# A time-warping front stage on Trainium2: where its norms are made, and in how many pieces its distances come

## The chip, the cores and the metric

The kernel runs on one core of a Trainium2 chip. The metric is device time in microseconds (us) from the first to the last instruction of one launch; the reported time is a median of several runs, beside one profiled execution from which all rows are taken. The engines are TensorE (PE, with its weight loads as PEld), VectorE (DVE), ScalarE (ACT), GpSimd (POOL) and SyncE (SP, which here only issues DMAs).

## The reference

The layer has four residual steps. Only the first is touched here: it aligns the context (4 batches of 1024 rows, 256 wide) with the layer-normed x (4 batches of 512 rows, 256 wide) by dynamic time warping.

```python
x = x + tanh(g_xattn[0]) * align(ctx_1024, layernorm(x))        # per batch:
    D = sqrt(max(aa + bb - 2 * small @ large.T, 0))               # small = ctx, large = normed x
    R[i, j] = D[i, j] + min(R[i-1, j], R[i, j-1], R[i-1, j-1])    # (1024, 512), in order
    path = backtrack(R)                                           # diagonal, up, left
    out[j] = sum of ctx rows on the path in column j
x = x + tanh(g_ffn[0]) * (attention, then mixture of experts)(layernorm(x))
x = x + tanh(g_xattn[1]) * cross_attention(layernorm(x), ctx_1024, mask)
x = x + tanh(g_ffn[1]) * fp4_ffn(layernorm(x))
```

Here `aa` and `bb` are the squared norms of the context rows and of the normed x rows.

## The kernel before

`load_all` brings in x and the context and turns the context so that its 256 features lie along partitions (`ctxT`). `dtw_block` (L159) then runs five blocks, and each ends with all engines waiting for each other:

1. `layer_norm` "ln0" (L51): DVE computes mean and variance of 16 groups of 128 rows, ACT takes the root, DVE writes the normed x.
2. `transpose_tokens` "xT" (L86): PE turns it, and it is kept times -2 as `xnT`.
3. `dtw_norms` (L181): twelve jobs of 512 columns. DVE squares (L234), PE sums the squares over partitions with a two-column weight (L248), DVE copies the sums out (L206). Eight jobs give the context norms, which go through DRAM (`ctx_norms`, L215 and L217) to be laid out as `norms`, one value per partition and row; four jobs give the norms of x, `rows_j`.
4. `dtw_costs` (L253): the distances and the recurrence.
5. `backtrack`.

In `dtw_costs` each partition holds a block of 33 context rows of one batch (32 blocks by 4 batches). The distances are made in pieces of up to 112 columns of x (`cuts`, L294). A piece has 33 tiles, one for each row of a block. For a tile PE does eight products (two halves of the features by four batches, each batch in its own 32 columns of the array, L333) and four more with two-row weights that add the norm of x (L336). A product of float32 is two instructions. Four PSUM banks take tiles in turn. Of the first piece DVE adds the context norm and clips at zero (L357) and ACT takes the root (L460). For all later pieces ACT does both: `rectify` (L449) for each tile, then four `root` (L456) over the piece, then `store` (L439) to `dist` in DRAM. Two SBUF buffers take the pieces in turn.

The recurrence walks 576 skewed columns in 36 chunks of 16 (`CH`). SP loads a chunk (L316) when the piece that holds it is stored (L313) and the chunk's buffer is free (L315), that is, just after the first column of the chunk before it. For each column DVE does a minimum (L378), a shuffle (L383) and a scan (L389), with pieces of `rule` (L348 to L351) between them that say which way the path came. After each chunk ACT copies these results out in `keep` (L430, L432). DVE may start the rules of chunk n only when ACT's `keep` of chunk n-2 is done (L403).

ACT's order of work is fixed in L463 to L473: in the chunks n = 0, 1, 2 of every four, eleven `rectify` ahead of the `keep` of that chunk; in the fourth, four `root` and the `store`.

```python
q, turn = 1 + n // 4, n % 4
if q < len(cuts) and turn < 3:
    for k in range(11):
        rectify(q * RB + 11 * turn + k)
elif q < len(cuts):
    for i in range(4):
        root(q, i)
    store(q)
act.wait_ge(coded, n + 1)
keep(1 - n % 2, n * CH)
```

Of the kernel before, what the change touches and what calls it, by code (L numbers as in the profile page):

```python
# [26 lines left out]
WIDE = 112  # L27
ITILE = SK // P
# [130 lines left out]
def dtw_block(nc, d, x_sb, ident, ctxT, ctxT_d):  # L159
# [3 lines left out]
    norms_d = nc.dram_tensor("ctx_norms", [1, B * PADI], F32).ap()  # L163
    with ExitStack() as es:
        near = es.enter_context(nc.sbuf_tensor("near", [P, RB, TROW], F16))
        above = es.enter_context(nc.sbuf_tensor("above", [P, RB, TROW], F16))
        with ExitStack() as es1:
            xnT = es1.enter_context(nc.sbuf_tensor("xnT", [P, DH, B * S], F32))
            with ExitStack() as es2:
# [4 lines left out]
            rows_j = es1.enter_context(nc.sbuf_tensor("rows_j", [2, B, S], F32))  # L174
            norms = es1.enter_context(nc.sbuf_tensor("norms", [P, RB], F32))
            dtw_norms(nc, d, xnT, ctxT, rows_j, norms, norms_d)
            dtw_costs(nc, d, dist, near, above, xnT, ctxT, ctxT_d, rows_j, norms, x_sb)
# [3 lines left out]
def dtw_norms(nc, d, xnT, ctxT, rows_j, norms, norms_d):  # L181

    with ExitStack() as es:
        sq = es.enter_context(nc.sbuf_tensor("sq", [P, 2, 2, 512], F32))
        ones2 = es.enter_context(nc.sbuf_tensor("ones2", [P, 2, 2], F32))
        add2 = es.enter_context(nc.sbuf_tensor("add2", [2, 2], F32))
        rows_i = es.enter_context(nc.sbuf_tensor("rows_i", [2, B, PADI], F32))
        ps_n = [es.enter_context(nc.psum_tensor(f"ps_n{i}", [P, 512], F32)) for i in range(2)]
        consts = es.enter_context(nc.semaphore("d_consts"))
        squared = es.enter_context(nc.semaphore("squared"))  # L190
        normed = es.enter_context(nc.semaphore("normed"))
        norm_kept = es.enter_context(nc.semaphore("norm_kept"))
        filled = es.enter_context(nc.semaphore("d_filled"))
        stored = es.enter_context(nc.semaphore("d_norms_stored"))
        spread = es.enter_context(nc.semaphore("d_norms_spread"))

        jobs = [(0, b, c, 1.0) for b in range(B) for c in range(0, SK, 512)] + [(1, b, 0, 0.25) for b in range(B)]
        with nc.Block() as block:
            def keep_norm(dve, n):
                w, b, c, f = jobs[n]  # L200
                if n == 0:
                    dve.wait_ge(consts, 32)
                    dve.wait_ge(filled, 2)
                dve.wait_ge(normed, n + 1)
                dst = rows_j[:, b, :] if w else rows_i[:, b, LEAD + c:LEAD + c + 512]
                nc.vector.tensor_scalar(dst, ps_n[n % 2][0:2, :], add2[:, w:w + 1], None,  # L206
                                        ALU.add).then_inc(norm_kept, 1)

            @block.sync
            def _(sp):  # L210
                sp.dma_start(ones2[:], d["c_ones2"]).then_inc(consts, 16)
                sp.dma_start(add2[:], d["c_add2"]).then_inc(consts, 16)
                sp.wait_ge(norm_kept, 2 * B)
                sp.wait_ge(filled, 2)
                sp.dma_start(norms_d, rows_i[0:1, :, :].rearrange("o b i -> o (b i)")).then_inc(stored, 16)  # L215
                sp.wait_ge(stored, 16)
                sp.dma_start(norms[:, :], norms_d.rearrange("o (p r) -> (o p) r", r=RB)).then_inc(spread, 16)  # L217
                sp.wait_ge(spread, 16)

            @block.gpsimd  # L220
            def _(pool):

                nc.gpsimd.memset(rows_i[:, :, :], 1.0).then_inc(filled, 1)
                pool.wait_ge(filled, 1)
                nc.gpsimd.memset(rows_i[0:1, :, 0:LEAD], FAR2).then_inc(filled, 1)

            @block.vector
            def _(dve):
                for n, (w, b, c, f) in enumerate(jobs):
                    if n >= 2:  # L230
                        dve.wait_ge(normed, n - 1)
                    for h in range(DH):
                        src = xnT[:, h, b * S:(b + 1) * S] if w else ctxT[:, b, h, LEAD + c:LEAD + c + 512]
                        i = nc.vector.scalar_tensor_tensor(sq[:, n % 2, h, :], src, f, src, ALU.mult, ALU.mult)  # L234
                    i.then_inc(squared, 1)
                    if n >= 1:
                        keep_norm(dve, n - 1)
                keep_norm(dve, len(jobs) - 1)

            @block.tensor  # L240
            def _(pe):
                pe.wait_ge(consts, 32)
                for n, (w, b, c, f) in enumerate(jobs):
                    pe.wait_ge(squared, n + 1)
                    if n >= 2:
                        pe.wait_ge(norm_kept, n - 1)
# [6 lines left out]
def dtw_costs(nc, d, dist, near, above, xnT, ctxT, ctxT_d, rows_j, norms, x_sb):  # L253
# [8 lines left out]
    with ExitStack() as es:  # L262
# [32 lines left out]
        with nc.Block() as block:  # L295
# [129 lines left out]
            def _(act):  # L425
# [36 lines left out]
                for n in range(NCH):  # L462
# [4 lines left out]
                    elif q < len(cuts):  # L467
                        for i in range(4):
                            root(q, i)
# [1819 lines left out]
```

## Time and profile before

| | us |
|---|---|
| median of 3 runs (2691.69 to 2695.81) | 2692.8 |
| profiled execution, its own time | 2694.47 |
| its span from first to last instruction | 2692.7 |

Of the span PE is busy 66%, DVE 61%, ACT 36%, POOL 10%. These shares are means over stages with different limits. The part that is touched lies in the first 510 us; the chain of work that ended last, on the page, is far behind it in the feed-forward step, and so the rows below are taken by stage.

### The profile page before, as it was taken

To read this page: it belongs to the slowest core of one execution; us is meant where nothing else is said; L and a number is where in the kernel's file an instruction comes from. 1 tells how busy PE (TensorE), PEld (TensorE's weight loads), DVE (VectorE), ACT (ScalarE), POOL (GpSimd) and SP (SyncE) were. 2 spreads that over 40 slices of the span, in tenths; PEclk is the share of its full clock that TensorE was granted. 3 is DMA by queue.
4 is the path that set the end of the run, shared out by engine and by line. 5 is a ranking of instruction groups with operands and counts; after the bars stand their busy time and mean duration, and the time that the engine had idled before them with its cause. 6 is when DMAs were issued, how large, how long until landed. Compare 5 with 4: busy or idle time off the path is not lost. (4 is left out here: it accounts for less than half of the span.)

```text
span 2692.7 us, 39964 instructions
## 1 busy us (share of the span) xinstructions
PE 1789.7 (66%) x13193; PEld 1032.5 (38%) x13272; DVE 1647.0 (61%) x6787; ACT 982.2 (36%) x1794; POOL 260.3 (10%) x224
## 2 busy tenths in 40 slices
PE   5989500170837888832979507999999999604675
PEld 2445300010724555421656405444544543303453
DVE  5397899898658888440101146767667676286544
ACT  1244522220015666500212002666666666313322
POOL 0000000000000000013000220000000000064432
PEclk8555555555958999955989857999999999857888
DMA  3211100300010000025041122100100000100000
GB/s 96 110 61 51 70 28 28 109 0 1 16 45 9 9 9 2 1 81 192 24 146 49 49 78 86 55 2 1 56 1 25 1 1 1 33 0 0 0 0 31
DMA packets 60244, 104.90 MB, mean 39 GB/s; under 512 B 7449, under 2 KB 42703, under 8 KB 58407
## 3 DMA queue, kind: packets, MB, share of 16 engines
q1 hardware_dynamic: 42654, 72.91, 7.9%
q10 hardware_dynamic: 14352, 22.28, 2.3%
q0 software_dynamic: 3072, 7.53, 0.9%
q8 instruction: 100, 1.64, 0.3%
q14 instruction: 66, 0.54, 0.1%
HBM read 70.72 MB, written 32.85 MB: 38 GB/s over the span
## 5 line engine op out<-in xcount | busy, mean ns | idle before, releaser
L1026 DVE CUSTOM_DVE_ANT_0 xam_junk<-xam_s,xa_mask_q 128x512 bf16<-128x512 f32 x512 | 339.7, 687 | 170.2 <-PE xam_s L933 169.6
L1099 ACT ACTIVATE xam_exp<-xam_s 128x512 f32<-128x512 f32 x512 | 299.6, 598 | 204.1 <-PE xam_s L967 167.6
L933 PE MATMUL xam_s<-xa_kT,xa_qT 96*128 96x512 bf16 x512 | 198.4, 391 | 16.6 <-DVE xam_max L1026 11.1
L964 PE MATMUL xam_s<-xa_qT,xa_kT 99*128 99x512 bf16 x512 | 196.9, 385 | 14.2 <-ACT xam_exp L1099 13.3
L635 PE MATMUL ps_e<-near,start_terms 128*128 128x512 f16 x66 | 27.7, 420 | 211.8 <-DMA lag<-c_lag 204.5
L967 PE MATMUL xam_s<-xa_mask_k,identb 128*128 128x512 bf16 x433 | 165.2, 381 | 0.0
L389 DVE TENSOR_TENSOR_SCAN cost<-m,cost,dist_chunk 128x33 f32<-128x33 f32 x576 | 164.1, 285 | 0.0
L333 PE MATMUL ps_d<-xnT,ctxT 128*32 128x112 f32 (+1 forms) x2640 | 151.5, 379 | 18.0 <-ACT stage L449 7.9
L1026 DVE CUSTOM_DVE_ANT_0 l0m_junk<-l0m_s,l_tri_q 128x128 bf16<-128x128 f32 (+3 forms) x256 | 118.7, 488 | 42.8 <-PE l0m_s L933 40.1
L978 PE MATMUL xam_o<-xam_exp,xa_vt 128*32 128x512 f32 x1024 | 137.2, 605 | 0.0
L1548 PE MATMUL ex_up<-ex_xT,ex_w 128*128 128x512 f32 x256 | 117.0, 616 | 17.6 <-DVE ex_xT L1580 12.0
L1099 ACT ACTIVATE l0m_exp<-l0m_s 128x512 f32<-128x512 f32 (+3 forms) x256 | 104.1, 439 | 60.9 <-PE l0m_s L967 59.3
L378 DVE TENSOR_TENSOR m<-cost 128x33 f32<-128x33 f32 x576 | 109.4, 190 | 20.8 <-DMA dist_chunk<-dist 14.0
L850 POOL COPY l_stk<-l_stk 128x256 bf16<-128x256 bf16 x32 | 21.0, 657 | 1012.1 <-DVE l_stk L829 1012.1
L1580 DVE TENSOR_SCALAR ex_xT<-ex_t,moe_vecs 128x512 f32<-128x512 f32 x16 | 12.2, 805 | 171.7 <-PE ex_t L1535 96.6
L333 PEld LDWEIGHTS ps_d<-xnT,ctxT 128*32 128x32 f32 x2640 | 90.6, 161 | 68.2 <-issue 45.9
L1559 PE MATMUL ex_dn<-ex_w,ex_hm 128*128 128x256 f32 x512 | 111.5, 379 | 0.0
L964 PEld LDWEIGHTS xam_s<-xa_qT,xa_kT 99*128 99x128 bf16 x512 | 50.7, 99 | 140.4 <-ACT xam_exp L1099 99.5
L933 PE MATMUL l0m_s<-l_kT,l_qT 96*128 96x128 bf16 (+3 forms) x256 | 79.8, 317 | 36.0 <-DVE l0m_max L1026 25.9
L1559 PEld LDWEIGHTS ex_dn<-ex_w,ex_hm 128*128 128x128 f32 x512 | 97.2, 191 | 13.6 <-issue 1.0
L430 ACT COPY near<-chunk_near 128x528 f16<-128x528 f16 x37 | 39.9, 1078 | 158.9 <-DVE chunk_near L351 157.3
L635 PEld LDWEIGHTS ps_e<-near,start_terms 128*128 128x128 f16 x66 | 6.8, 102 | 228.5 <-DMA lag<-c_lag 204.7
(324 smaller groups left out, 3900.4 us busy)
## 6 DMA issues: line engine op xcount, KB each, us to landing
dist_chunk<-dist SPq DMA_DIRECT2D x36, 264.0 KB
ex_w<-L_ffn_W ACTq DMA_DIRECT2D x8, 1024.0 KB, 15.1
ex_w<-L_ffn_W SPq DMA_DIRECT2D x8, 1024.0 KB, 16.3
xa_mask<-mask_BxSxS_ik SPq DMA_DIRECT2D x4, 2048.0 KB, 11.1
ctx_nat<-ctx ACTq DMA_DIRECT2D x4, 1024.0 KB, 14.5
x_sb<-x SPq DMA_DIRECT2D x2, 2048.0 KB, 12.3
ctxT_d<-ctxT SPq DMA_DIRECT2D x4, 1024.0 KB, 9.5
ctx_rows<-ctx SPq DMA_DIRECT2D x1, 4096.0 KB, 15.5
```

Source lines behind the costliest of these rows:

```text
L333: nc.tensor.matmul(o[b], ctxT[:, b, h, k:PADI:RB], xnT[:, h, b * S + a:b * S + z], start=(h == 0), stop=False, tile_position=(0, 32 * b))
L378: nc.vector.tensor_tensor(m[:, u, :], w[:, src, 0:RB], w[:, src, 1:PITCH], ALU.min).then_inc(minned[h], 1)
L389: nc.vector.tensor_tensor_scan(w[:, dst, 1:PITCH], m[:, u, :], step[h][:, s, :], w[:, dst, 0:1], ALU.min, ALU.add).then_inc(scanned[h], 1)
L430: nc.scalar.copy(near[:, :, bass.ds(at, CH)], kept_n[buf][:, :, :].rearrange("p s r -> p r s"))
L933: nc.tensor.matmul(ps1[n % 2][:, 0:w], qT[0:STK, slot(g, h), qt * P:(qt + 1) * P], kT[0:STK, slot(g, h), f * 512:f * 512 + w], start=True, ...
L964: nc.tensor.matmul(o[:, q0:512], kT[:, slot(g, h), kt * P:(kt + 1) * P], qT[:, slot(g, h), q0:512], start=True, stop=False)
L967: nc.tensor.matmul(o[:, q0:q0 + w], identb[:, :], heads.bias_k(g, kt), start=False, stop=True).then_inc(scored2, 1)
L978: nc.tensor.matmul(pso[32 * h:32 * h + 32, q0:512], vt[:, kt, slot(g, h), :], ebuf[n % NE][:, q0:512], start=(kt == 0), stop=(kt == kt_n - 1),
L1026: nc.vector.tensor_tensor_reduce(junk[:, n % NJ, 0:w], ps1[n % 2][:, 0:w], heads.bias_q(g, qt, f), 1.0, NEG * 4, ALU.add, ALU.max, mx[:, g ...
L1099: nc.scalar.activation(ebuf[at % NE][:, q0:512], ps2[at % 2][:, q0:512], ACT.Exp).then_inc(exped, 1)
L1548: last = nc.tensor.matmul(pu[k % 4][:, :], w1[i][:, h, c * P:(c + 1) * P], xT[i % 2][:, h, :], start=(h == 0), stop=(h == DH - 1))
L1559: last = nc.tensor.matmul(pd[k % 2][:, 0:D], hm[i % 2][:, c, t * P:(t + 1) * P], w2[i][:, c, :], start=(c == 0), stop=(c == FC - 1))
```

## The change

- `layer_norm` and the context half of `dtw_norms` become one block, `norm_inputs`. POOL squares the context (eight instructions of 128x1024), PE sums them with a weight that puts each batch's sum on its own partition (`c_which`), ACT copies the sums out, SP stores them and reads them back as `norms`; DVE does the layer norm in the same block. SP does not wait there for the read-back; DVE does, in `dtw_costs`.
- The squares of xnT are made at the head of `dtw_costs`, by four DVE instructions of 128x1024, after PE has been given the feature products of the first four tiles. PE sums them by sixteen instructions, ACT copies the sums to `rows_j` (4x512).
- The norm of x is added to a tile by one product with a 4x128 weight (`c_share`) for all batches, in place of four with 2x32 weights.
- `m` and `cost` are preset by POOL in place of DVE.
- The pieces are 48, 64, 80, 96, 112 and 112 columns wide. The first is stored in two parts, 16 and 32 columns.
- ACT's work on a piece is spread evenly over the chunks of the piece before it.

```diff
+WIDTHS = (48, 64, 80, 96, 112, 112)
+STORES = (0, 16, 48, 112, 192, 288, 400)
...
-                layer_norm(nc, es2, x_sb, xn, "ln0")
+                with ExitStack() as es3:
+                    norm_inputs(nc, es3, d, x_sb, xn, ctxT, which, rows_i, norms, norms_d, spread)
...
-            dtw_norms(nc, d, xnT, ctxT, rows_j, norms, norms_d)
...
+def norm_inputs(nc, es, d, x_sb, xn, ctxT, which, rows_i, norms, norms_d, spread):
...
+            sp.dma_start(which[:, :, :], d["c_which"]).then_inc(known, 16)
+            sp.wait_ge(filled, 1)
+            sp.wait_ge(kept, 2)
+            sp.dma_start(norms_d, rows_i[:, :]).then_inc(stored, 16)
+            sp.wait_ge(stored, 16)
+            sp.dma_start(norms[:, :], norms_d.rearrange("b (p r) -> (b p) r", r=RB)).then_inc(spread, 16)
...
+            for n, (b, h) in enumerate(jobs):
+                if n >= 4:
+                    pool.wait_ge(weighed, n - 3)
+                src = ctxT[:, b, h, LEAD:PADI]
+                nc.gpsimd.tensor_tensor(sq[:, n % 4, :], src, src, ALU.mult).then_inc(squared, 1)
...
+                pe.wait_ge(squared, n + 1)
+                for c in range(2):
+                    last = nc.tensor.matmul(ps[c][0:B, :], which[:, b, :], sq[:, n % 4, c * 512:(c + 1) * 512],
+                                            start=(n == 0), stop=(n == len(jobs) - 1))
+                last.then_inc(weighed, 1)
...
+            act.wait_ge(weighed, len(jobs))
+            for c in range(2):
+                nc.scalar.copy(rows_i[:, LEAD + c * 512:LEAD + (c + 1) * 512], ps[c][0:B, :]).then_inc(kept, 1)
...
+        for q in range(1, len(cuts)):
+            first, turns = cuts[q - 1][0] // CH - 1, WIDTHS[q - 1] // CH
+            items = [("rectify", q * RB + k) for k in range(RB)] + [("root", (q, i)) for i in range(4)] + [("store", q)]
+            for i, item in enumerate(items):
+                work[first + i * turns // len(items)].append(item)
...
-                    for b in range(B):
-                        last = nc.tensor.matmul(o[b], one_j[:, :], rows_j[:, b, a:z], start=False, stop=True,
-                                                tile_position=(0, 32 * b))
-                    last.then_inc(prod, 1)
+                def close(n):
+                    a, z = cuts[n // RB]
+                    nc.tensor.matmul(ps[n % 4][:, 0:z - a], share[:, :], rows_j[:, a:z], start=False,
+                                     stop=True).then_inc(prod, 1)
+                for n in range(4):
+                    tiles(n)
+                for b in range(B):
+                    pe.wait_ge(squared, b + 1)
+                    for h in range(DH):
+                        last = nc.tensor.matmul(ps_j[0:B, :], which[:, b, :], squares[:, b, h * S:(h + 1) * S],
+                                                start=(b == 0 and h == 0), stop=(b == B - 1 and h == DH - 1))
+                last.then_inc(normed, 1)
+                pe.wait_ge(told, 16)
+                pe.wait_ge(jnormed, 1)
+                for n in range(4):
+                    close(n)
+                for n in range(4, len(cuts) * RB):
+                    tiles(n)
+                    close(n)
...
-                nc.vector.memset(w[:, :, :], FAR).then_inc(blank, 1)
-                nc.vector.memset(m[:, :, :], FAR).then_inc(blank, 1)
+                for b in range(B):
+                    src = xnT[:, :, b * S:(b + 1) * S]
+                    nc.vector.scalar_tensor_tensor(squares[:, b, :].rearrange("p (h s) -> p h s", h=DH), src, 0.25, src,
+                                                   ALU.mult, ALU.mult).then_inc(squared, 1)
+                dve.wait_ge(spread, 16)
...
+                act.wait_ge(normed, 1)
+                nc.scalar.copy(rows_j[:, :], ps_j[0:B, :]).then_inc(jnormed, 1)
...
                 store(0)
+                prepare(-1)
                 for n in range(NCH):
...
+                    prepare(n)
                     act.wait_ge(coded, n + 1)
                     keep(1 - n % 2, n * CH)
```

`prepare(n)` does the items of `work[n]` in order.

## Rows read from the trace of the kernel before

**Rows 1.** Busy time of each engine by stage: start:end length, engines, clock, DMA.
```profile
46.50:75.50 29.00, 24.01 (x48) 3.35 (x48) 23.81 (x37) 0.00 (x0) 3.80 (x2) 0.94 0.01 1
75.50:124.10 48.60, 48.52 (x812) 26.35 (x816) 15.13 (x35) 13.43 (x33) 0.00 (x0) 0.50 0.28 111
124.10:137.60 13.50, 13.50 (x228) 7.22 (x232) 0.00 (x0) 4.18 (x10) 0.00 (x0) 0.50 0.42 163
137.60:509.30 371.70, 160.05 (x2928) 89.63 (x2928) 340.68 (x2970) 133.54 (x209) 0.00 (x0) 0.50 0.13 45
509.30:2692.70 2183.40, 1527.31 (x9089) 890.06 (x9168) 1246.96 (x3685) 821.13 (x1528) 255.98 (x217) 0.84 0.10 34
```

**Rows 2.** What DVE waited for in the loop: us in total, times, longest.
```profile
DVE best L348 <- ACT above L432: 24.2, 5, 5.9
DVE m L378 <- DMA dist_chunk<-dist: 14.0, 1, 14.0
```

**Rows 3.** Timeline of ACT in the loop: start, duration, line, shapes, idle before.
```profile
209.03 0.47 ACT L449 ACTIVATE x_sb<-ps_d,norms 128x112 f32<-128x112 f32 x1 [0.98 <-PE ps_d L336]
210.72 1.07 ACT L430 COPY near<-chunk_near 128x528 f16<-128x528 f16 x1
...
403.52 1.07 ACT L430 COPY near<-chunk_near 128x528 f16<-128x528 f16 x1 [7.74 <-DVE chunk_near L351]
...
422.82 1.07 ACT L430 COPY near<-chunk_near 128x528 f16<-128x528 f16 x1 [7.75 <-DVE chunk_near L351]
```

**Rows 4.** Timeline of PE: tiles of 112 columns, then of 64.
```profile
75.58 0.98 PE L333 MATMUL ps_d<-xnT,ctxT 128*32 128x112 f32 x16 [2.27 <-DMA one_j<-c_one_j]
76.50 0.60 PE L336 MATMUL ps_d<-rows_j,one_j 2*32 2x112 f32 x8
77.02 0.98 PE L333 MATMUL ps_d<-xnT,ctxT 128*32 128x112 f32 x16
...
276.71 0.66 PE L333 MATMUL ps_d<-xnT,ctxT 128*32 128x64 f32 x16
277.30 0.44 PE L336 MATMUL ps_d<-rows_j,one_j 2*32 2x64 f32 x8
277.67 0.66 PE L333 MATMUL ps_d<-xnT,ctxT 128*32 128x64 f32 x16
```

**Rows 5.** Timeline of the blocks ahead of the distances.
```profile
26.55 5.32 DVE L66 BATCH_NORM_STATS2 ln_stats<-x_sb 128x6 f32<-128x256 f32 x16 [1.01 <-PEq L48]
...
39.28 6.40 PE L118 MATMUL xT_ps<-ident,dtw_xn 128*128 128x128 f32 x32 [14.03 <-PEq L61]
...
46.63 2.50 DVE L234 SCALAR_TENSOR_TENSOR sq<-ctxT 128x512 f32<-128x512 f32 x4 [0.66 <-PEq L96]
...
48.23 5.29 PE L248 MATMUL ps_n<-sq,ones 128*2 128x512 f32 x8 [2.54 <-DMA add<-c_add]
...
53.93 3.74 PE L248 MATMUL ps_n<-sq,ones 128*2 128x512 f32 x8 [0.41 <-DVE sq L234]
...
66.30 0.23 SPq L215 DMA_DIRECT2D ctx_norms<-rows_i  x1
...
67.99 0.35 SPq L217 DMA_DIRECT2D norms<-ctx_norms  x1
```

**Rows 6.** POOL's products of two tensors by shape: count, busy us, mean ns.
```profile
L1905 POOL TENSOR_TENSOR ffq_sgn<-ffq_sgn,ffq_amax 128x1024 f32<-128x1024 f32 x4 | 10.8, 2689 | 0.0
...
L1901 POOL TENSOR_TENSOR ffq_v<-ffw_xn,ffq_inv 128x1024 f32<-128x1024 f32 x4 | 8.7, 2176 | 8.6 <-DVE ffq_inv L1876 8.6
```

**Rows 7.** Timeline: first store, first load, first column of the recurrence.
```profile
124.13 0.35 ACTq L439 DMA_DIRECT2D dist<-x_sb  x1
...
132.08 0.62 SPq L316 DMA_DIRECT2D dist_chunk<-dist  x1
...
137.63 0.20 DVE L378 TENSOR_TENSOR m<-cost 128x33 f32<-128x33 f32 x1 [13.96 <-DMA dist_chunk<-dist]
```

**Rows 8.** ACT's roots over a piece of 64 columns, grouped by shape.
```profile
L456 ACT ACTIVATE x_sb<-x_sb 128x528 f32<-128x528 f32 x4 | 2.2, 625 | 0.0
```

More of the change, by code:

```diff
@@ L173, in dtw_block @@
                 transpose_tokens(nc, es2, xn, lambda g, h: xnT[:, h, g * 512:(g + 1) * 512], ident, "xT", mul=-2.0)
-            rows_j = es1.enter_context(nc.sbuf_tensor("rows_j", [2, B, S], F32))
-            norms = es1.enter_context(nc.sbuf_tensor("norms", [P, RB], F32))
-            dtw_norms(nc, d, xnT, ctxT, rows_j, norms, norms_d)
-            dtw_costs(nc, d, dist, near, above, xnT, ctxT, ctxT_d, rows_j, norms, x_sb)
+            dtw_costs(nc, d, dist, near, above, xnT, ctxT, ctxT_d, which, norms, spread, x_sb)
@@ L178, in dtw_block @@
         backtrack(nc, d, near, above, spans, x_sb, ident)
[L181 to L246, printed above, removed]
-                    for h in range(DH):
-                        last = nc.tensor.matmul(ps_n[n % 2][0:2, :], ones2[:, w, :], sq[:, n % 2, h, :],
-                                                start=(h == 0), stop=(h == DH - 1))
-                    last.then_inc(normed, 1)
@@ L262, in dtw_costs @@
+def dtw_costs(nc, d, dist, near, above, xnT, ctxT, ctxT_d, which, norms, spread, x_sb):
     with ExitStack() as es:
@@ L456, in root, with prepare @@
                     nc.scalar.activation(part, part, ACT.Sqrt).then_inc(rooted, 1)
+                def prepare(n):
+                    for kind, arg in work[n]:
+                        if kind == "rectify":
+                            rectify(arg)
+                        elif kind == "root":
+                            root(*arg)
+                        else:
+                            store(arg)
                 for k in range(RB):
                     act.wait_ge(clipped, k + 1)
-                    nc.scalar.activation(stage[0][:, :, k], stage[0][:, :, k], ACT.Sqrt).then_inc(rooted, 1)
+                    nc.scalar.activation(stage[0][:, 0:WIDTHS[0], k], stage[0][:, 0:WIDTHS[0], k],
+                                         ACT.Sqrt).then_inc(rooted, 1)
                 store(0)
+                prepare(-1)
                 for n in range(NCH):
-                    q, turn = 1 + n // 4, n % 4
-                    if q < len(cuts) and turn < 3:
-                        for k in range(11):
-                            rectify(q * RB + 11 * turn + k)
-                    elif q < len(cuts):
-                        for i in range(4):
-                            root(q, i)
-                        store(q)
+                    prepare(n)
                     act.wait_ge(coded, n + 1)
```

102 lines of the change are left out of this document (77 added, 25 removed).

## The prediction

> **What bounds the kernel now.** I read the busy time by stage first [rows 1]. The part that changes ends at 509.3; the 2183.4 us behind it share no instruction with the edit, so I carry them over unchanged. Ahead of that point there are two kinds of lost time. Up to 137.6 the recurrence has not begun: the norms take 29.0 us, the first piece of distances 48.6 with PE busy for 48.52, and 13.5 go to its store and first load, DVE at zero. From 137.6 to 509.3 DVE carries the recurrence, busy for 340.7 of 371.7.
>
> The waits of DVE say what is lost inside the loop [rows 2]: 24.2 us for ACT's `keep`, in five waits; the 14.0 for the first load are the stretch ahead of the loop. ACT's timeline says why [rows 3]: eleven `rectify` stand in front of a `keep`, and each waits 0.98 us for PE. The reader is to see that ACT works 0.47 us for each tile and the rest of its time is PE's. Where nothing waits, two chunks take 422.82 - 403.52 = 19.30, so 9.65 each; 36 of them make 347.4, and with 24.2 that is the loop's 371.6.
>
> PE's price for a tile [rows 4]: 1.44 us at 112 columns (0.92 for the eight feature products, 0.52 for the four norm products), 0.96 at 64 (0.59 and 0.37). Through both goes 0.32 + 0.010 per column: 0.80 at 48, 1.12 at 80, 1.28 at 96.
>
> **The change part by part.** All from the profiled execution, whose own time is 2694.47, 1.7 above the median shown.
>
> *Norms ahead of the distances.* The new block starts where the layer norm did, 26.55 [rows 5]. Its longest chain is POOL's: eight products of 128x1024. Two rows bound one, 2.18 and 2.69 [rows 6]; I take 2.3, near the first, since both operands are one tile: 18.4 us, to 45.2 with the preset (bounds 44.2 and 48.3). The layer norm's 12.7 us on DVE (26.55 to 39.28) lie beside it; were POOL and DVE to hold each other up for all of DVE's last pass, about 5 us would be added. Behind POOL come the last four sums on PE, 1.9 (half of 3.74 for eight), two ACT copies of 512 columns at 0.6 (a 528-element row is 0.625 [rows 8]), and SP's store with the issue of the read-back, 67.99 + 0.35 - 66.30 = 2.0 [rows 5]: 50.3, and with a block turn 50.6. This block is 11.3 us later at its end than the layer norm was. SP no longer waits for the read-back; DVE does, ahead of its 33 clips, but it lands some 15 us before the first tile, so nothing queues there. The transposes keep 46.63 - 39.28 = 7.35: `dtw_costs` starts at 57.9.
>
> Then PE does four feature halves (4 x 0.48 = 1.9) while DVE squares (8 x 0.625 = 5.0 in four steps of 1.25). PE's sixteen sums take 7.5 at the full clock, 2.4 GHz (twice 3.74), and 13.6 at the half, 1.2 GHz (0.85 each); a first group of eight in 5.29 shows both levels [rows 5]. I take 7.5, since dense transposes run directly before. ACT's copy, for which all closes wait, costs 0.8: 68.4. Four feature halves are then already done, so it is as if tile 0 had begun at 66.5, where it began at 75.58: 9.1 gained (bounds 10 and 0, with POOL's rows and the clock's two levels). Presets moved to POOL free 1.9 us of DVE that PE's sums cover anyway; SP's copies of `ctxT` and the presets' DMAs moved 0.28 x 48.6 = 13.6 us' worth in the first piece's stretch [rows 1]; they start with the block at 57.9 and are done long before the first store.
>
> *The one close for four.* No row shows a 4x128 product between column tiles. The old norm products cost 0.15 us beyond their columns; below, that goes to nothing with two instructions for eight (-0.15 a tile). Above, two loads of 128 columns lie open: a transpose instruction with such a load and 128 columns takes 0.20 [rows 5], half of it load, so +0.2. I take no change, the tile as before, as the streamed columns are the same number.
>
> *The pieces.* Tile 33 ends at 66.5 + 33 x 0.80 = 92.9; clip, root and issue bring the store to 93.9. A store of 112 columns took 7.95 [rows 7]; for 16 columns I take 2.6 (in proportion 1.1, but even a small store takes 1.7 [rows 5]; above 7.95). The load takes 137.63 - 132.08 = 5.55. The loop starts at 102.0, not 137.6. Of these 35.6, 9.1 are the norms, 21.1 the narrower piece, 5.3 the store.
>
> Piece 1 must be there for chunk 3, due at 102.0 + 28.9 = 130.9. PE ends it at 92.9 + 33 x 0.96 = 124.6; the last `rectify` 0.5, four roots 2.5 [rows 8], a store of 64 columns 4.5 (in proportion), the load 5.55: 137.6. Chunk 3 is late by 6.7. Piece 2, for chunk 7, due at 176.2: 124.6 + 37.0 + 1.0 of PE waiting on ACT + 0.5 + 3.0 + 5.7 + 5.55 = 177.3, late by 1.1. Piece 3 comes 4 us early for chunk 12, pieces 4 and 5 early or just in time, since PE needs at most 7.9 us of a chunk's 9.65 from there on. `keep` is late no more: in chunk 0, the tightest, 26 tiles of piece 1 stand before it, to 92.9 + 26 x 0.96 = 117.9, and with 2.2 it is done at 120.1, where chunk 2 begins at 121.3; from chunk 2 on ten items or fewer stand before one. So the 24.2 go and 7.8 come.
>
> *Sum.* 102.0 + 347.4 + 7.8 = 457.2 for 509.3: 52.1 gained, 2642.4, or 2640.7 on the median. Forecast 2641.
>
> **Rivals.**
>
> *The clock stays up.* PE was all but fully busy on tiles of 32 columns at half clock for 48.6 us [rows 1], so these tiles don't raise it. But they began there just after PE had stood idle for 2.27 us [rows 4]; now they would follow dense sums closely, 0.9 us apart. If the clock holds through two pieces, tiles cost 0.40 and 0.48: tile 33 ends at 78.7, the loop starts at 87.9, piece 1 is in time, and 87.9 + 347.4 = 435.3: 2620. Against it: narrow tiles with DVE and ACT in turn leave gaps. The Trainium skill, "TensorE: Matmul & The Clock Gate", section "What's actually happening", says that the throttled state is the default and activity releases it; by that rule alone 2620 would be likely, but the 48.6 us above disagree with it for this kind of tile.
>
> *The close drains the array.* Each tile now changes from four column tiles to the whole array and back, 396 times. Price: both loads open, +0.2 a tile. By chunk 7 that is 99 x 0.2 = 19.8 on 177.3, so 197.1; the 29 chunks left take 279.9: 477.0, and about 2 at chunk 12: 2664. With half of it, 2654. Against it: the old pair changed between 128-row and 2-row weights as often, at 1.44 in all. The Trainium skill, "TensorEngine Tiling (Array Packing)", section "Key Properties", says that a change of tiling mode drains the engine; no row here shows such a drain by itself.
>
> *Slower than before.* Place: PE between the last feature product and the close of each tile. If a tile costs 0.45 more, pieces 0 to 4 end 165 x 0.45 = 74 us later on PE. Piece 4 without that: 66.5 + 33 x (0.80 + 0.96 + 1.12 + 1.28 + 1.44) + 5 + 0.5 + 3.9 + 7.95 + 5.55 = 274.2, and 18 chunks behind it, 173.7: 447.9. With 74 it is 522: 2707. It decides from (509.3 - 447.9) / 165 = 0.37 a tile, nearly twice what two open loads cost.
>
> *It doesn't do what it says.* The loop keeps waiting for `keep` as before, 24.2 for the 7.8: 2659. Against it: of 112 columns at most seven stand before a `keep`, not eleven, and PE runs four tiles ahead; but chunk 0 has 1.2 us to spare only.
>
> **How the numbers follow.** Forecast 54% (2632 to 2652, from the front's bounds and -0.15 to +0.05 a tile), clock up 21% (2614 to 2632), drain or late `keep` 20% (2652 to 2672), slower 4%, no change 1%. The range 2616 to 2663 holds the first, most of the second and over half of the third. What a measurement can tell from no change is 0.2%, 5.4 us; all but the last two cases are faster by more: faster 0.95, same 0.01, slower 0.04.
>
> **What would show it.** POOL's eight products near 2.3 us and ending near 45; transposes from near 50.6; the first close near 68.5; tiles 0.80 us apart in the first piece and 1.44 at 112 columns, clock 0.50; the first column at 102; DVE waiting for a load, not for ACT, about 7 us near chunk 3 and hardly at all later; loop end near 457. Tiles 0.40 apart show the clock's rival, 1.0 or more in the first piece the drain. I am wrong if tiles at 112 columns exceed 1.8 us, if DVE still waits over 15 us in the loop, or if the stretch behind the loop is not 2183 within 5.

## The result, and the profile after

The changed kernel takes 2671.66 us (median of 4 runs, 2668.73 to 2674.33) where the kernel before, run beside it, takes 2693.6: a ratio of 0.9918, 95% interval 0.9901 to 0.9935. That is 22 us faster; 52 were forecast, and 2671.7 lies above the range. The profiled execution is 2674.33 long. Its stages, to be read beside [rows 1] (start:end length, busy time of PE, PEld, DVE, ACT, POOL, clock, DMA share, GB/s):

```profile
53.70:62.81 9.11, 8.26 (x80) 2.47 (x81) 4.63 (x4) 0.57 (x1) 1.96 (x2) 1.00 0.67 266
62.81:95.00 32.19, 32.19 (x547) 26.09 (x547) 9.71 (x33) 9.24 (x33) 0.00 (x0) 0.54 0.23 92
95.00:102.50 7.50, 7.50 (x110) 5.77 (x110) 0.00 (x0) 2.27 (x6) 0.00 (x0) 0.50 0.40 146
102.50:472.80 370.30, 230.94 (x2846) 160.97 (x2845) 340.44 (x2970) 145.86 (x249) 0.00 (x0) 0.50 0.13 48
472.80:2672.20 2199.40, 1544.65 (x9168) 895.32 (x9168) 1247.38 (x3686) 822.31 (x1528) 255.69 (x217) 0.83 0.10 34
```

The loop starts at 102.5 (102.0 forecast) but takes 370.3 instead of 355.2, so it ends at 472.8 (457.2 forecast, 509.3 before), and the stretch behind it is 2199.4 instead of 2183.4, in code that the change doesn't touch. DVE still has 340.4 us of work in the loop; what it waits for is this, to be read beside [rows 2]:

```profile
DVE m L419 <- DMA dist_chunk<-dist: 26.1, 4, 9.6
DVE best L386 <- ACT above L475: 4.9, 1, 4.9
```

The 26.1 are 7.8 ahead of the loop, then 9.6, 6.9 and 1.8 for chunks 3, 7 and 12. The blocks ahead of the loop, beside [rows 5]:

```profile
26.47 14.99 POOL L222 TENSOR_TENSOR ctx_sq<-ctxT 128x1024 f32<-128x1024 f32 x8
34.51 10.97 DVE L249 TENSOR_SCALAR dtw_xn<-x_sb,ln_mv,ln_rstd 128x256 f32<-128x256 f32 x16
47.45 5.35 PE L120 MATMUL xT_ps<-ident,dtw_xn 128*128 128x128 f32 x32 [3.73 <-PEq L205]
55.03 7.03 PE L367 MATMUL ps_j<-x_sb,which_batch 128*4 128x512 f32 x16
62.81 0.39 PE L359 MATMUL ps_d<-rows_j,share 4*128 4x48 f32 x2 [0.76 <-ACT rows_j L469]
```

And a tile of 112 columns, beside [rows 4]:

```profile
301.98 0.98 PE L353 MATMUL ps_d<-xnT,ctxT 128*32 128x112 f32 x16
302.89 0.50 PEld L359 LDWEIGHTS ps_d<-rows_j,share 4*128 4x128 f32 x2 [0.33 <-issue]
302.89 0.76 PE L359 MATMUL ps_d<-rows_j,share 4*128 4x112 f32 x2
303.58 0.58 PEld L353 LDWEIGHTS ps_d<-xnT,ctxT 128*32 128x32 f32 x16 [0.20 <-issue]
303.58 0.98 PE L353 MATMUL ps_d<-xnT,ctxT 128*32 128x112 f32 x16
```

The close is what finishes a tile, the product of `share` that adds the norm of x. From the start of the features' products to the close it is 0.91 us, as before; the close takes 0.69 where the four took 0.52, so 1.61 a tile for 1.44. At 48, 64, 80 and 96 columns the tiles come 1.07, 1.21, 1.34 and 1.47 us apart: 0.27, 0.25, 0.22 and 0.19 more than forecast. Only the first six ran at the full clock, the fifth and sixth 0.74 apart; at 65.3 the granted clock fell to 0.50, and it stayed there for the rest of the loop.

### The profile page after: what moved, and what is told of

The parts are those of the page before. It is cut to its first block and busy times, and to the rows that moved or that the text cites. A ratio compares the mean times of both kernels' runs of the same rounds, so it can differ in the third digit from the quotient of the medians.

```text
span 2672.2 us, 39247 instructions
## 1 busy us (share of the span) xinstructions
PE 1854.2 (69%) x12876; PEld 1108.5 (41%) x12876; DVE 1629.2 (61%) x6753; ACT 991.3 (37%) x1834; POOL 273.3 (10%) x233
## 5 line engine op out<-in xcount | busy, mean ns | idle before, releaser
L1016 PE MATMUL xam_s<-xa_qT,xa_kT 99*128 99x512 bf16 x512 | 196.7, 384 | 13.7 <-ACT xam_exp L1151 12.9
L1019 PE MATMUL xam_s<-xa_mask_k,identb 128*128 128x512 bf16 x512 | 195.3, 381 | 0.0
L353 PE MATMUL ps_d<-xnT,ctxT 128*32 128x112 f32 (+4 forms) x3168 | 158.1, 348 | 9.8 <-ACT stage L497 8.4
L359 PE MATMUL ps_d<-rows_j,share 4*128 4x112 f32 (+4 forms) x396 | 140.5, 456 | 0.8 <-ACT rows_j L469 0.8
L1600 PE MATMUL ex_up<-ex_xT,ex_w 128*128 128x512 f32 x256 | 122.9, 641 | 21.9 <-DVE ex_xT L1632 12.6
L419 DVE TENSOR_TENSOR m<-cost 128x33 f32<-128x33 f32 x576 | 109.6, 190 | 32.6 <-DMA dist_chunk<-dist 26.1
L359 PEld LDWEIGHTS ps_d<-rows_j,share 4*128 4x128 f32 x396 | 96.9, 303 | 49.0 <-issue 45.7
L353 PEld LDWEIGHTS ps_d<-xnT,ctxT 128*32 128x32 f32 x3168 | 97.1, 160 | 40.1 <-issue 17.4
```

Source lines behind the costliest of these rows:

```text
L353: nc.tensor.matmul(ps[n % 4][32 * b:32 * b + 32, 0:z - a], ctxT[:, b, h, k:PADI:RB], xnT[:, h, b * S + a:b * S + z], start=(h == 0), stop= ...
L359: nc.tensor.matmul(ps[n % 4][:, 0:z - a], share[:, :], rows_j[:, a:z], start=False, stop=True).then_inc(prod, 1)
L419: nc.vector.tensor_tensor(m[:, u, :], w[:, src, 0:RB], w[:, src, 1:PITCH], ALU.min).then_inc(minned[h], 1)
L1016: nc.tensor.matmul(o[:, q0:512], kT[:, slot(g, h), kt * P:(kt + 1) * P], qT[:, slot(g, h), q0:512], start=True, stop=False)
L1019: nc.tensor.matmul(o[:, q0:q0 + w], identb[:, :], heads.bias_k(g, kt), start=False, stop=True).then_inc(scored2, 1)
L1600: last = nc.tensor.matmul(pu[k % 4][:, :], w1[i][:, h, c * P:(c + 1) * P], xT[i % 2][:, h, :], start=(h == 0), stop=(h == DH - 1))
```

## The experiments

Two questions: what makes the close dear, and where the 16 us behind the loop come from. "Stretch" is the time from the loop's last column to the end of the span.

**e1, four closes again.**

```
-                    nc.tensor.matmul(ps[n % 4][:, 0:z - a], share[:, :], rows_j[:, a:z], start=False,
-                                     stop=True).then_inc(prod, 1)
+                    for b in range(B):
+                        last = nc.tensor.matmul(ps[n % 4][32 * b:32 * b + 32, 0:z - a], share[:, 32 * b:32 * b + 32],
+                                                rows_j[:, a:z], start=False, stop=True, tile_position=(0, 32 * b))
+                    last.then_inc(prod, 1)
```

> The changed kernel with one edit: each tile of distances is closed by four products, one a batch, each of 32 columns of share (its four rows long) into its own 32 partitions, in place of one product of all 128 columns; everything else is as in the changed kernel. Theory (the whole-array product is what costs: its tile pitch was 1.07, 1.21, 1.34, 1.47 and 1.61 us at 48, 64, 80, 96 and 112 columns against 0.96 at 64 and 1.44 at 112 before): the pitch comes back to about 0.80, 0.96, 1.12, 1.28 and 1.44 us, the loop still starts near 102, its wait for chunk 3 falls from 9.6 to about 7 us and that for chunk 7 from 6.9 to about 1, and it ends near 450 instead of 472.8; the total is 2650, give or take 8 for the stretch behind the loop (2183 to 2199). Rival (the dearer tile comes from something else that changed in these pieces, for instance the sums of x in four rows instead of two, or the order of work on ScalarE): the pitch stays and the total is 2671.

Measured: 2650.1, tiles 0.80, 0.96, 1.12, 1.28 and 1.44 apart, loop 100.6 to 453.0, stretch 2195.7. At 112 columns:

```profile
291.83 0.98 PE L353 MATMUL ps_d<-xnT,ctxT 128*32 128x112 f32 x16 [2.53 <-ACT stage L499]
292.74 0.60 PE L360 MATMUL ps_d<-rows_j,share 4*32 4x112 f32 x8
293.27 0.98 PE L353 MATMUL ps_d<-xnT,ctxT 128*32 128x112 f32 x16
```

The whole-array close alone costs 19.8 us of loop end and 21.5 of the total. The stretch stays long, so the close is not its cause.

**e4, paired closes, and e6, closes of 64 columns.** In e4 `tiles(n); tiles(n + 1); close(n); close(n + 1)` replaces `tiles(n); close(n)`; in e6 the loop of e1 runs over two halves of 64 columns.

> The changed kernel with the products of each two tiles put together: eight products of features for tile n, eight for n+1, then the two closes, from the fifth tile on. The number and shape of the products stay. T1 (going over between products of 32 columns of the array and one of all its columns costs a fixed time, once each way): a pair pays it once instead of twice, and two tiles take 0.15 to 0.3 us less together than twice the pitch of now (2.95 at 48: about 1.95 to 2.0 instead of 2.15; at 112 about 3.0 instead of 3.21); the loop ends near 461. T2 (each close pays for loading its own 128 columns of weights before it, which nothing hides): the pair takes what two single tiles took, 2.15 at 48 and 3.21 at 112 within 0.05, and the loop ends within 2 of 472.8.

Measured: 2655.9, loop end 459.7. A pair takes 1.82 us at 48 columns and 2.78 at 112, which is 0.33 and 0.43 less than two tiles of the changed kernel: more than T1's 0.15 to 0.3, where T2 gave nothing. So a change of shape does cost something. But the second close of a pair adds 0.43 at every width, which T1 doesn't explain. Two closes at 112 columns, up to the next features:

```profile
303.02 0.93 PEld L359 LDWEIGHTS ps_d<-rows_j,share 4*128 4x128 f32 x4 [0.33 <-issue]
303.02 1.19 PE L359 MATMUL ps_d<-rows_j,share 4*128 4x112 f32 x4
304.14 1.33 PEld L353 LDWEIGHTS ps_d<-xnT,ctxT 128*32 128x32 f32 x32 [0.20 <-issue]
```

Each f32 product is two passes (two records a close), and from the second on they follow each other by 0.213 at 48 as at 112 columns: the columns streamed don't set this pace. The 128 columns of weights that each pass loads are the same at both widths; e6 tries whether it is they that do.

> The changed kernel with each tile closed by two products of 64 columns of share, one for each half of the partitions. The paired closes gave 0.213 us from pass to pass of a 128-column close whatever its width. T2' (what is paid is the loading of the close's columns: the first load lies open behind the features' products, the second sets the pitch of the second pass; 0.213 us for 128 columns at the low clock, so 0.107 for 64 and 0.053 for 32): a tile costs 0.05 more than with four closes, and at 48 columns 0.03 more, so 0.88, 1.01, 1.17, 1.33 and 1.49 us at 48, 64, 80, 96 and 112 columns; the loop ends near 457. T1 (what is paid is a fixed price of going from 32 columns to more and back): the tile stays near 1.07, 1.21, 1.34, 1.47 and 1.61 and the loop ends near 473.

Measured: 2653.2, loop end 454.6 (457 expected), tiles 0.87, 1.00, 1.16, 1.32 and 1.48 apart, where T2' gave 0.88 to 1.49 and T1 1.07 to 1.61.

```profile
293.54 0.98 PE L353 MATMUL ps_d<-xnT,ctxT 128*32 128x112 f32 x16 [2.33 <-ACT stage L499]
294.45 0.64 PE L360 MATMUL ps_d<-rows_j,share 4*64 4x112 f32 x4
295.02 0.98 PE L353 MATMUL ps_d<-xnT,ctxT 128*32 128x112 f32 x16
```

So what a close costs beyond its columns goes by the columns of weights loaded, as T2' has it: the first load lies open, the second holds the second pass back. The Trainium skill, "TensorE: Matmul & The Clock Gate", section "LDWEIGHTS (loading the stationary operand)", says that the load's time goes by the columns and not by the contracted rows; e1, e6 and the changed kernel, with 32, 64 and 128 columns, agree as to the columns; the rows were 4 in all three.

**e3, equal pieces** (WIDTHS 112, 112, 112, 112, 64, one store each, one close a tile) **and e8, the same with four closes.**

> The changed kernel with the pieces of before: 112, 112, 112, 112 and 64 columns, each stored by one transfer; norms and closes as in the changed kernel. Theory (the dear close takes back what the graded pieces bring): the first store leaves some 22 us later, the loop starts near 124.6 instead of 102.5, has no wait for a chunk any more, and ends near 471.6, within 3 of the changed kernel's 472.8; tile pitch 1.607 us at 112. Total 2655 to 2672 by the stretch behind the loop (2183 to 2199). Rival (the graded pieces still bring what they were forecast to, about 30 us): the loop ends near 500.

Measured: 2662.0, loop 125.0 to 472.0 without a wait. The changed kernel's loop ends at 472.8: under the dear close the graded pieces bring nothing. Yet this kernel is 9.6 us faster, nearly all of it behind the loop (2189.8).

> The changed kernel with the pieces of before (112, 112, 112, 112 and 64 columns, one store each) and four closes a tile: of the change only the norms and their place are left. Expected from the two single edits: tile pitch 1.44 at 112 columns, loop start 119.5 (125.0 with equal pieces and one close, less 33 tiles by 0.167), no wait for a chunk, loop end 466.5. The graded pieces are then worth 13.5 us with four closes (466.5 to 453.0) and nothing with one (472.0 and 472.8). Rival (the start of the loop is not set by the tiles but by ScalarE's and VectorE's own work on the first piece): loop start 124 or later. Total 2650 to 2665 by the stretch behind the loop; if equal pieces are what keeps that stretch short (2188 with them, 2194 to 2197 with graded pieces), 2656.

Measured: 2653.4, loop 123.2 to 469.9 (119.5 and 466.5 expected), stretch 2184.7. So the norms' new place and ScalarE's new work list, which this kernel keeps too, bring 39 us of loop end: 14 by the earlier start, and 25 in the loop, where no `keep` is waited for any more, although the pieces and the tile's 1.44 us are as before. The likely reason is the work list, which here puts five or six items ahead of each `keep`, where eleven tiles stood ahead of three in four; no run has the one without the other. The graded pieces add 17 with four closes.

**e2 and e5, a pause behind the loop.** A block in which VectorE fills 2048 columns of a scratch tensor, in the changed kernel and in the kernel before.

> The changed kernel with an idle block between the loop and the walk back: VectorE fills 2048 columns of a scratch tensor (about 1.8 us at the rate of the 1920-column fill, 1658 ns, plus the ends of a block), and all the other engines wait. No work is changed in what follows. Theory P (the 16 us that the code behind the loop took longer, 2199.4 against 2183.4 us, come from when its matmul bursts fall against the changes of TensorE's granted clock, so that they move with any delay): the stretch behind the loop, less the pause, comes out several us away from 2199.4, in either direction, and the total with it. Rival (the change costs the code behind it a fixed amount, by something it leaves behind): the stretch less the pause is 2199.4 within 2 and the total is the changed kernel's plus the pause, 2674 to 2676.

> The kernel before with the same idle block between the loop and the walk back as in the paused changed kernel (VectorE fills 2048 columns of a scratch tensor). In the runs so far the stretch behind the loop, the median time less what lies ahead of it, is 2182.6 us before, 2196.7 in the changed kernel, 2195.0 with four closes a tile, 2194.1 with paired closes, 2188.2 with equal pieces. Theory P (the stretch depends on when its matmul bursts fall against the changes of the granted clock): a shift alone makes it longer here too, by 3 us or more beyond the pause, median 2699 or more. Rival (something in the changed kernel makes it longer, whatever the shift): the kernel before keeps its 2183 and becomes 2696 (2693.84 and the pause of 2.3) within 2.

Measured: 2674.2 (2670.8 to 2683.6) and 2696.9 (2695.0 to 2700.7). By the medians a shift costs little more than it lasts, 2.6 and 3.5 us; the long stretch doesn't go away in the one or come in the other. So theory P doesn't explain why the stretch is long. The four runs of e2 lie 13 us apart, though, so some scatter of this kind is there.

**e9, seven stores, and e11, five on ScalarE's queue.** In the traces so far the stretch was long in the kernels with graded pieces and seven stores, and most of the time was lost in the experts' stage, where ScalarE issues sixteen transfers of weights ahead of its gelu, in two groups of eight ("issues" below is the time that each group takes to issue). e9 is e8 with STORES = (0, 16, 112, 224, 336, 400, 448).

> The kernel of e8 (equal pieces, four closes a tile) with seven stores of distances in place of five: cut also at columns 16 and 400, as many transfers as the changed kernel sends by ScalarE's queue. The traces of all five kernels with seven stores show the eight pairs of weight transfers of the experts' stage (2.3 MB, issued on ScalarE's queue 800 us later) issued in 24.8 to 26.2 us, and those of the four kernels with five stores in 21.4 to 23.6 us; gelu waits for the last issue, TensorE for gelu. Theory Q (the number of stores on ScalarE's queue decides how its later issues are held up): the issues take 25 us, the stretch behind the loop goes from 2184.7 to 2194, the loop ends near 469 and the total is 2664. Rival R (it is the number of tiles or the length of the program, 198 tiles against 161 or 165): the issues stay at 22 us, the stretch at 2185, the total at 2654. Rival P (only the time at which the bursts fall against the changes of the clock): either, but without the change in the issues.

Measured: 2662.6, loop end 466.0, issues 24.6 and 25.7 us, stretch 2194.9: theory Q. e11 is the changed kernel with two stores moved from ScalarE to SyncE (shortened):

```
+   sp.wait_ge(rooted, RB)          # SyncE, ahead of the first load
+   sp.dma_start(dist[:, ...], stage[0][...]).then_inc(stored[j], 16)    # j = 0 and 1
```

> The changed kernel with the two stores of the first piece (columns 0 to 16 and 16 to 48) issued by SyncE in place of ScalarE: seven stores as before, five of them on ScalarE's queue. Loop start 102.5 and loop end 472.8 within 1.5. Theory Q1 (the number on ScalarE's own queue decides): the experts' weights on ScalarE's queue are issued in about 22 us in the pattern of five stores (5, 10 and 4 us at the fourth, sixth and eighth), the stretch behind the loop is about 2186, and the total 2660. Theory Q2 (the number of store transfers in all decides, on whichever queue): the issues take 25 us, the stretch stays at 2195 to 2199 and the total at 2671.

Measured: 2658.7, loop 101.8 to 472.2, issues 23.3 and 21.3, stretch 2184.5: theory Q1 (2186 and 2660 expected). The second group of weights on ScalarE's queue in the changed kernel (start, time of the issue), then in e11:

```profile
1361.62 4.48 ACTq L1567 DMA_DIRECT2D ex_b<-L_ffn_b  x1
1366.26 0.66 ACTq L1564 DMA_DIRECT2D ex_w<-L_ffn_W  x1
1367.08 4.69 ACTq L1567 DMA_DIRECT2D ex_b<-L_ffn_b  x1
1371.94 6.59 ACTq L1564 DMA_DIRECT2D ex_w<-L_ffn_W  x1
1378.68 6.40 ACTq L1567 DMA_DIRECT2D ex_b<-L_ffn_b  x1
1385.18 1.28 ACT L1576 ACT_TABLE_LOAD   x1 [57.78 <-issue]
```

```profile
1353.09 4.61 ACTq L1576 DMA_DIRECT2D ex_b<-L_ffn_b  x1
1357.86 0.39 ACTq L1573 DMA_DIRECT2D ex_w<-L_ffn_W  x1
1358.41 8.08 ACTq L1576 DMA_DIRECT2D ex_b<-L_ffn_b  x1
1366.66 1.46 ACTq L1573 DMA_DIRECT2D ex_w<-L_ffn_W  x1
1368.28 4.38 ACTq L1576 DMA_DIRECT2D ex_b<-L_ffn_b  x1
1372.75 1.28 ACT L1585 ACT_TABLE_LOAD   x1 [53.89 <-issue]
```

ScalarE is held in its own eight issues for 25.2 us (from 1359.87) instead of 21.3 (from 1351.34), so its gelu starts late, and TensorE, whose four banks of products are full, waits (changed kernel, then e11; idle before in brackets; the last row of each is the stretch behind the wait, with PE, PEld, DVE, ACT, POOL, granted clock and DMA):

```profile
1373.31 10.18 PE L1600 MATMUL ex_up<-ex_xT,ex_w 128*128 128x512 f32 x16 [4.54 <-DVE ex_xT L1632]
1387.21 6.19 PE L1600 MATMUL ex_up<-ex_xT,ex_w 128*128 128x512 f32 x7 [3.72 <-ACT ex_hm L1576]
1387.20:1393.40 6.20, 6.19 (x8) 2.69 (x9) 0.00 (x0) 2.38 (x4) 0.00 (x0) 0.52 0.63 201
```

```profile
1364.25 8.65 PE L1609 MATMUL ex_up<-ex_xT,ex_w 128*128 128x512 f32 x16 [4.26 <-DVE ex_xT L1641]
1374.79 5.42 PE L1609 MATMUL ex_up<-ex_xT,ex_w 128*128 128x512 f32 x12 [1.89 <-ACT ex_hm L1585]
1374.80:1380.20 5.40, 5.40 (x13) 2.53 (x14) 0.00 (x0) 3.04 (x5) 0.00 (x0) 1.00 1.09 351
```

It waits 3.7 instead of 1.9, and behind the longer wait its products run at a granted clock of 0.52 and 0.88 us apart (7 in 6.19), behind the shorter at 1.00 and 0.45 apart (12 in 5.42). From the first issue of this group to the end of the span the changed kernel takes 1312.3 us and e11 1305.4. The first group loses in the same way: from its first issue to that of the second it is 143.5 and 140.4.

**e10 and e12, six and four stores on ScalarE's queue.** e10 is the changed kernel without the cut at 16, e12 is e8 with its first store issued by SyncE.

> The changed kernel with its first piece stored by one transfer of 48 columns instead of two of 16 and 32: six stores. The loop starts some 1 us later (the store of 48 columns lands 3.4 us after its issue, that of 16 after 2.1) and ends at 472 to 474. Theory Q: the stretch behind the loop changes by some microseconds from 2196.7, in a direction that five and seven stores don't tell; the issues of the experts' weights show another pattern than 4.9, 6.7 and 5.8 us. Rival R: the same pattern, 2196.7 and a total of 2671 to 2673.

> The kernel of e8 (equal pieces, four closes a tile, five stores) with the first store issued by SyncE: four stores on ScalarE's queue. Loop end 470. Theory Q1: the issues of the experts' weights show a third pattern; their sum may be 22 or 25 us (five gave 22, six, seven and eight gave 25), and if the rule is 'few are good' it stays at 22 with a total of 2653. Theory Q2 (five in all): 22 us, the pattern of five stores, 2653.

Measured: e10 2671.4, loop end 471.7, issues 25.5 and 25.5 in another pattern (the longest single issue 10.3 us, 6.7 in the changed kernel), stretch 2198.1; e12 2658.5, loop end 465.5, issues 24.7 and 24.5, stretch 2190.8. Few is not good: with four, six and seven the issues take 25 us, with five 22. Two further versions, both with four closes, give eight and five:

> Seven pieces of 48, 48, 64, 64, 80, 96 and 112 columns, eight stores, four closes a tile of 32 columns, the products of two tiles put together: an attempt at a faster version. The loop starts at 100.6 as with paired tiled closes (there ScalarE's and VectorE's own work on the first piece takes over from TensorE), has no wait and ends near 447.5. By theory Q the stretch behind it is not known for eight stores: 2184 to 2196, total 2634 to 2646.

> Five pieces of 80, 96, 112, 112 and 112 columns, five stores, four closes a tile: the graded start with as few stores as before. The loop starts near 111, has no wait for a chunk and ends near 458. Theory Q: with five stores the experts' weights are issued in 22 us and the stretch is 2184.7, total 2645. Rival R (198 tiles or the graded pieces decide; here there are 165 tiles): also 2645; rival P: 2645 to 2655.

Measured: best2 2640.7, loop 97.2 to 444.4, issues 25.7 and 24.8, stretch 2199.3; best4 2645.6, loop 114.0 to 461.1 (111 to 458 expected), issues 22.8 and 21.7, stretch 2186.9. The kernel before happened to stand at five. Why five, no run shows.

The stretch is read best in two parts, up to the first of these issues (at 1247.40 in the kernel before, 1216.33 in the changed one, 1210.98 in e11) and from it to the end of the span:

| | stores on ScalarE's queue | loop end to first issue | first issue to end |
|---|---|---|---|
| before | 5 | 738.1 | 1445.3 |
| e8 | 5 | 739.1 | 1445.6 |
| e11 | 5 | 738.8 | 1445.7 |
| best4 | 5 | 741.3 | 1445.7 |
| e3 | 5 | 741.4 | 1448.4 |
| e12 | 4 | 738.2 | 1452.6 |
| e9 | 7 | 739.2 | 1455.7 |
| changed kernel | 7 | 743.5 | 1455.9 |
| e10 | 6 | 742.1 | 1456.0 |
| best2 | 8 | 743.3 | 1456.0 |

The second part goes by the stores, about 10 us between five and six or more. The first does not: with seven stores it is as short as 739.2 (e9), with five as long as 741.4 (e3). Of the 16.0 us by which the changed kernel's profile is longer behind the loop, 10.6 belong to the queue; the other 5.4 lie ahead of these issues, where the traces scatter, and what makes them scatter is open.

**e7 and the versions built on it.** e7 is e1 with the tiles in pairs.

> The changed kernel with four closes a tile (32 columns each) and the products of each two tiles put together: features of n and n+1, closes of n and n+1, from the fifth tile on. In the trace with four closes a tile takes six passes of w/600 us and 0.32 us besides, of which the trace shows 0.15 to 0.16 at each of two places, into the close and out of it. Theory (the 0.16 is paid where products of one shape follow products of another, so that it is there in the kernel before too): a pair takes 12 passes and 0.32 once: 1.28, 1.60, 1.92, 2.24 and 2.56 us at 48, 64, 80, 96 and 112 columns, the loop starts near 95 and ends near 440, and the total is 2638 give or take 6. Rival (the 0.16 belongs to each accumulation group, that is to each tile): a pair takes 1.60 to 2.88 and the loop ends near 453 as with four closes.

Measured: 2645.2, loop 100.6 to 447.5. Pairs come 1.28 to 2.56 apart, as in the theory, so 0.16 is paid at each change from products of one shape to another, and most likely in the kernel before too, whose tile of 1.44 is that of e1. But the loop starts 5 late: the first close comes at 65.5 (62.8 in the changed kernel), and TensorE stops for 3.95 in the first piece. It also stops in the same kernel with two stores by SyncE:

> The changed kernel's pieces and seven stores with four closes a tile and paired tiles (2645.2 with loop end 447.5), its first two stores issued by SyncE, five on ScalarE's queue. Loop end 447 to 448. Theory Q1: weights issued in 22 us, stretch 2186, total 2635. Theory Q2: 25 us, total 2645.

Measured: 2632.1, loop 97.2 to 444.0, issues 22.9 and 21.3, stretch 2185.5. Its TensorE in the first piece:

```profile
64.60 0.34 PE L362 MATMUL ps_d<-xnT,ctxT 128*32 128x48 f32 x6
68.90 0.80 PE L362 MATMUL ps_d<-xnT,ctxT 128*32 128x48 f32 x26 [3.97 <-issue]
70.10 0.88 PE L362 MATMUL ps_d<-xnT,ctxT 128*32 128x48 f32 x32
```

It stops amid the features of a pair, with nothing to wait for that the profile shows, while the copy of the transposed context (4 MB) fills the DMA engines. From 65 to 69 they are 96% busy with it (packets, MB, share of the 16 engines):

```profile
q1 hardware_dynamic: 409, 1.55, 96.1%
q8 instruction: 1, 0.02, 1.5%
```

The second row is a queue that brings instructions. A third version of this kind missed its loop end:

> The version with seven graded pieces, eight stores, four closes a tile and paired tiles (2640.7 with loop end 444.4 and 2199 behind it), with its first three stores issued by SyncE, so that five stay on ScalarE's queue. Loop end 444 to 446. Theory Q1: weights issued in 22 us, stretch 2186, total 2631. Theory Q2: 25 us, 2195 to 2199, total 2641.

Measured: 2636.2, stretch 2184.2 as expected, but loop end 448.5: SyncE, waiting to send the third store, is late with chunk 2's load, and VectorE waits 5.3 us.

The last version is the one of 2632.1 with that copy moved behind the loads of chunks 26, 28, 30 and 32.

> The version with paired tiles and five stores on ScalarE's queue (2632.1; loop 97.2 to 444.0), with the four transfers that copy the transposed context to memory (1 MB each) moved from ahead of the loop to behind the loads of chunks 26, 28, 30 and 32. In six traces with closes in tiles TensorE stood still for 2.3 to 4.0 us in the first piece, waiting for nothing but instructions, until about when these transfers ended. Theory: its instructions come by transfers that queue behind them; without them the stop of 3.97 us goes, the loop starts near 93.2, has no wait and ends near 440, total 2628. Rival (the stop is of the program itself): it stays, the loop ends near 444, total 2632; a chunk load held up by the moved copies would show as a wait of VectorE behind chunk 26.

Measured: 2627.1, ratio 0.9753 (0.9737 to 0.9769), loop 92.9 to 440.0 with no wait in it, and no stop (here the window of the view ends at 66.5, within the last row):

```profile
64.77 1.26 PE L363 MATMUL ps_d<-xnT,ctxT 128*32 128x48 f32 x32
66.44 0.32 PE L363 MATMUL ps_d<-xnT,ctxT 128*32 128x48 f32 x4
```

So the copy causes the stop. That TensorE waits for its instructions is the likely way, as the instructions' queue brings nothing from 60 to 65 with the copy there and one packet of 16 KB without it; no run tests it by itself.

**e13, the changed kernel with both cures.**

> The changed kernel with both single cures: four closes of 32 columns a tile, and the two stores of the first piece issued by SyncE (five on ScalarE's queue). If the two causes add up and there is no third: loop end 453.0, stretch behind it 2184.5, total 2639.6 give or take 3, against the forecast of 2641 made without either. If they overlap or a third cause is there, the total is 2645 or more.

Measured: 2641.0 (2638.1 to 2644.2), loop 97.8 to 452.0, stretch 2184.6. The two causes add up, and no third shows beyond the 3 us that the expectation allows.

## Why the prediction was wrong, step by step

- *The one close for four: "I take no change, the tile as before, as the streamed columns are the same number".* This step failed. A term put at nothing measured +0.17 us a tile at 112 columns and +0.27 at 48. The upper bound, two loads open, had the right mechanism, and at +0.2 throughout it was too low for the narrow pieces. In sum the close costs 21.5 us of the total (e1). The row I leaned on, that the columns streamed are the same, says nothing of loads; the first product behind features of another shape doesn't hide its load of 128 columns, and the second pass waits for its own (0.213 us from pass to pass in e4).
- *The stretch behind the loop: "share no instruction with the edit, so I carry them over unchanged", within 5.* This step failed as well: +16.0 in the profile. Two more stores on ScalarE's queue change how its later issues are held, which is 10.6 of it; with five on that queue e11 is back at 1445.7 from the first issue to the end. I counted where the stores land, and not what they do to the queue that they use. The other 5.4 are of the scatter ahead of these issues, for which the prediction allowed 5 us. So the 12.9 us that e11 gives back of the total are partly that scatter.
- *The norm block.* Right in mechanism, but ready 5.6 us sooner than forecast: POOL's products take 1.87 us and not 2.3, the block's store is issued at 44.89, and the first close comes at 62.8 (68.4 forecast, where the parts named add to 68.1). DVE's last pass is held up by 5.7, where I had put about 5, but ends at 45.5, before the transposes.
- *Loop start 102.0.* Measured 102.5. That it came so near is luck, two errors that nearly cancel: the front is 5.6 early, the tiles of the first piece are late (27 at 1.07 instead of 0.80 is 7.3).
- *The pieces.* Chunk 3 late by 9.6 (6.7), chunk 7 by 6.9 (1.1), chunk 12 by 1.8 (0), and one `keep` of 4.9 that the dear tiles bring back. With four closes and five stores (e13) chunks 3 and 7 are late by 6.2 and 0.7, near the forecast. Its total of 2641.0 is the forecast too, in part by luck, as its loop starts 4.2 sooner than forecast.
- *Rivals.* The drain's (2664, +0.2 a tile) came nearest: its loop end was 477.0, measured 472.8. A change of shape costs 0.16 by itself (e7), but the old close most likely paid that too; what is new is the load. The Trainium skill, "TensorEngine Tiling (Array Packing)", section "Key Properties", says that a change of tiling mode drains the engine; no run here shows whether the 0.16 is such a drain. The clock did not stay up: six tiles, then 0.50. The loop did still wait for a `keep`, once, for 4.9 of the 24.2 us before.

## What to carry to other kernels

A product of all the array's columns between products of few pays for loading its columns twice (f32), at the narrowest piece most; count the columns loaded, not only those streamed. A transfer added to an engine's queue can cost time far behind it, where the same engine issues many: compare the issue times of that queue, engine by engine, in all stages. Before you call a change in an unchanged stage noise or clock, set its rows beside each other and cut it where the two begin to differ: here 10.6 us had a cause, with the clock as a consequence, and 5.4 were scatter of which no run shows the cause.

## What the runs showed of the hardware

- The issues of eight weight transfers on ScalarE's queue took 21.3 to 23.6 us with five stores sent ahead, 24.5 to 26.2 with four, six, seven or eight, some 800 us later.
- TensorE stood still for up to 3.97 us (best6) while a copy of 4 MB filled the DMA engines, waiting for nothing that the profile shows, and no longer when the copy was moved (best7). The changed kernel itself has no such stop.
- DVE's last pass of the norms (16 instructions of 128x256) took 10.97 us beside POOL's products, where the same pass took 5.26 in the kernel before with POOL idle. The loss is all in the first four instructions: the last three of these take 5.78, one for each product of POOL that is left, and the twelve behind POOL's last product 3.95. The Trainium skill, "SBUF — State Buffer", section "SBUF: two separate sides", says that the two engines share a pair of ports as an exclusive lock for the whole instruction; the trace agrees: these three end at 37.81, 39.70 and 41.60, each just behind the end of a product of POOL (37.66, 39.56, 41.45), and the twelve run 0.32 us apart, as in the kernel before.

```profile
33.87 7.58 POOL L222 TENSOR_TENSOR ctx_sq<-ctxT 128x1024 f32<-128x1024 f32 x4
35.83 5.78 DVE L249 TENSOR_SCALAR dtw_xn<-x_sb,ln_mv,ln_rstd 128x256 f32<-128x256 f32 x3
41.53 3.95 DVE L249 TENSOR_SCALAR dtw_xn<-x_sb,ln_mv,ln_rstd 128x256 f32<-128x256 f32 x12
```
